# Pooled conditioning, attention and a mixture of experts on one core: block 0's first units weigh their rows last, weights come in 512 KB transfers, score banks are freed earlier, and the halves of the even blocks' input lie elsewhere

## What is computed

```python
# pooling of the tokens of a sequence; a mask of three kinds
scores = tanh(x @ W1 + b1) @ v
p = softmax(where(mask, scores[:, None, :], NEG_INF))
pooled = einsum('bjl,bld->bjd', p, x) / cnt
# attention, 16 heads of 8, one rope part of 32 for all heads
c_kv = pooled @ W_kv_down
k, v = c_kv @ W_k_up, c_kv @ W_v_up
k_rope = rotary(c_kv @ W_k_rope)
q, q_rope = pooled @ W_q, rotary(pooled @ W_q_rope)
w = softmax(causal((q k^T + q_rope k_rope^T) / scale))
x = x + (w @ v) @ W_o
# experts
xc = x @ W[cat_ids] + b[cat_ids]
tidx, tw = gate(xc)          # sigmoid, 4 of 8 groups, the best 8 of 64, normed, times 2.5
y = sum over e of cw[:, e] * ((silu(xc @ We_gate[e]) * (xc @ We_up[e])) @ We_down[e])
y = y + (silu(xc @ Ws_gate) * (xc @ Ws_up)) @ Ws_down
x = x + y
```

## Time and profile before

| | |
|---|---|
| median of 3 runs (lowest, highest) | 727.07 us (725.82, 727.83) |
| the profiled execution | 730.47 us |
| its span in the trace | 728.6 us |
| mean granted clock of PE | 0.988 |
| PE busy | 704.1 us (97%) |
| PEld busy | 547.9 us (75%) |
| DVE busy | 543.2 us (75%) |
| ACT busy | 444.0 us (61%) |
| POOL busy | 424.5 us (58%) |
| HBM read, written | 88.37 MB, 3.15 MB |

### The profile page before, as it was taken

How to read it: one execution, slowest core, us unless ns; L and a number is a source line. 1 busy time by engine, 2 the same in 40 slices (tenths; PEclk the granted TensorE clock), 3 DMA queues, 4 the chain that set the end, 5 groups by cost and what they waited for, 6 DMA issues and landing times.

```text
span 728.6 us, 15761 instructions
## 1 busy us (share of the span) xinstructions
PE 704.1 (97%) x5616; PEld 547.9 (75%) x5616; DVE 543.2 (75%) x1146; ACT 444.0 (61%) x857; POOL 424.5 (58%) x351
## 2 busy tenths in 40 slices
PE   7989889999999999999999999999999999999997
PEld 5767668677887778777787778877787777888885
...
GB/s 257 107 113 124 202 149 112 124 104 163 106 124 114 145 109 121 138 101 146 120 112 137 107 157 105 126 113 140 113 125 138 97 150 115 110 129 142 128 130 46
DMA packets 66845, 92.93 MB, mean 128 GB/s; under 512 B 7888, under 2 KB 26768, under 8 KB 66768
## 3 DMA queue, kind: packets, MB, share of 16 engines
...
HBM read 88.37 MB, written 3.15 MB: 126 GB/s over the span
## 4 chain that ended last, share of the span: by engine, by line
PE 74%; DVE 10%; ACT 5%; SPq 4%; issue 4%; DMA 2%; POOL 1%; POOLq 0%; DVEq 0%; ACTq 0%
PE banks L997 71%; DVE hid L964 3%; DVE hid L976 2%; PE banks L1077 2%; DVE k_blk L693 1%; DVE pt_sb L668 1%; SPq L302 1%; ACT banks L531 1%; SPq L296 1%; DMA x_early<-in_x_feat 1%; SPq L272 1%; ACT s_t L405 1%; ACT hid_hi L543 1%; SPq L333 1%; ACT v_blk L392 1%
## 5 line engine op out<-in xcount | busy, mean ns | idle before, releaser
L640 POOL TENSOR_TENSOR hid_lo<-hid,hid_hi 128x512 fp32r<-128x512 f32 (+1 forms) x264 | 342.1, 1296 | 261.1 <-ACT hid_hi L543 259.3
L964 DVE TENSOR_TENSOR hid<-banks,cwb 128x512 f32<-128x512 f32 x254 | 174.6, 687 | 122.1 <-ACT banks L531 115.1
L531 ACT ACTIVATE banks<-banks 128x512 f32<-128x512 f32 x254 | 147.4, 582 | 134.3 <-PE banks L997 132.7
L543 ACT CAST hid_hi<-hid 128x512 fp32r<-128x512 f32 (+1 forms) x264 | 162.7, 616 | 78.7 <-DVE hid L976 76.9
L976 DVE TENSOR_TENSOR hid<-hid,banks 128x512 f32<-128x512 f32 (+1 forms) x264 | 181.4, 687 | 25.3 <-PE banks L997 2.9
L997 PE MATMUL banks<-c_hi,wg_hi 128*128 128x512 f32 x264 | 118.9, 450 | 4.6 <-DVE hid L964 3.4
L997 PE MATMUL banks<-hid_hi,wd_hi 128*128 128x512 f32 (+1 forms) x264 | 104.6, 396 | 0.8 <-POOL hid_lo L640 0.8
L997 PE MATMUL banks<-c_hi,wg_lo 128*128 128x512 f32 x264 | 104.0, 394 | 0.0
L997 PE MATMUL banks<-c_lo,wg_hi 128*128 128x512 f32 x264 | 104.0, 394 | 0.0
L997 PE MATMUL banks<-hid_hi,wd_lo 128*128 128x512 f32 (+1 forms) x264 | 103.7, 393 | 0.0
L997 PE MATMUL banks<-hid_lo,wd_hi 128*128 128x512 f32 (+1 forms) x264 | 103.6, 393 | 0.0
...
## 6 DMA issues: line engine op xcount, KB each, us to landing
cwb<-cw_scratch SPq DMA_DIRECT2D x254, 256.0 KB, 3.8
...
xf<-in_x_feat SPq DMA_DIRECT2D x8, 256.0 KB, 3.9
out_feat<-y ACTq DMA_DIRECT2D x8, 256.0 KB, 3.4
wg_raw<-in_we_gate SPq DMA_DIRECT2D x7, 256.0 KB, 4.7
wu_raw<-in_we_up SPq DMA_DIRECT2D x7, 256.0 KB, 4.5
wd_raw<-in_we_down SPq DMA_DIRECT2D x7, 256.0 KB, 4.5
xf<-in_x_tok SPq DMA_DIRECT2D x6, 256.0 KB, 2.7
```

What stands on the lines that cost most here:

```text
L531: nc.scalar.activation(dst, gate_bank(p)[:, :], ACT.Silu).then_inc(S["silu_done"], 1)
L543: nc.scalar.copy(hid_hi[0:n, slot(b, p), :], hid[0:n, slot(b, p), :]).then_inc(S["hi_ready"], 1)
L640: nc.gpsimd.tensor_sub(hid_lo[0:n, slot(b, p), :], hid[0:n, slot(b, p), :], hid_hi[0:n, slot(b, p), :].bitcast(F32)).then_inc(S["lo_ready" ...
L964: nc.vector.tensor_mul(hid[:, slot(b, p), :], gate, weight)\
```

## The change

In eight parts:

1. **First loads.** `x_feat` 0 is second on SP's queue, was fourth. `consts` moves to ACT's. The seven other loads of `x_feat` and `x_tok` 1 move from ACT's queue to SP's.
2. **Weights in 512 KB.** `weight_pair` loads eight pairs of experts at once, 12 transfers in place of 24. ACT issues those of the first pair of quarters, SP seven more and the shared expert's ahead of block 0's units, and the last two down parts ahead of the first cwb. None stands between two cwb any more.
3. **Prologue order.** PE's `pool_scores(1)` goes from ahead of `pool_out(0)` to behind step 0, DVE's to step 5; ACT's splits 0 and 1 go to step 4; warming products are 5 and 2 where there were 2, 6 and 2, and 7 where there were 9.
4. **Rows weighed last in units 0 to 3 of block 0.** ACT puts silu 0 to 3 into `hid`; DVE multiplies by up first (`gate_up`) and by the weights second; the gates of units 2 and 3 stand ahead of the transposition of the weights, their ups behind the `pick` products. These go to Y and A1 (`first_bank`).
5. **Two tiles at once.** DVE (and POOL) do steps 6 and 7 behind unit 1 and 8 and 9 behind unit 3 (`TWO_TILES`); PE's step 8, the second round of scores, goes from unit 3 to unit 4 (`SECOND_ROUND`). `pool_weights(2)` goes from unit 6 to unit 5.
6. **Splits.** 8 in place of 10 ahead of the units; then one behind each of units 6 to 17, and 20 to 24 behind units 24 to 28. `CHAIN` goes from 25 to 21.
7. **Score banks.** A semaphore `score_read` at the addition of the mask (L714) replaces `biased_tile`, at the maximum (L715), in the waits of step 8, of the first transposition in step 12 and of up 6. Before, the addition and the maximum followed each other by a wait too.
8. **Address.** c_hi0 and c_lo0 are declared right behind `wd_hi`.

The diff, cut:

```diff
@@ -109,6 +109,7 @@
         hid_hi, hid_lo = sb("hid_hi", [P, NH, TOK], F32R), sb("hid_lo", [P, NH, TOK], F32R)
         wg_hi, wu_hi = sb("wg_hi", [P, UNITS, P], F32R), sb("wu_hi", [P, NPAIR, P], F32R)
         wd_hi = sb("wd_hi", [P, UNITS, D], F32R)
+        c_hi0, c_lo0 = sb("c_hi0", [P, TOK], F32R), sb("c_lo0", [P, TOK], F32R)
...
-        c_hi = [sb("c_hi0", [P, TOK], F32R), c_hi1]
-        c_lo = [sb("c_lo0", [P, TOK], F32R), c_lo1]
+        c_hi, c_lo = [c_hi0, c_hi1], [c_lo0, c_lo1]
...
+        first_bank = [Y, A1]
...
+        def steps_behind(p, b, prev, moved, last=False):
+
+            if not prev and p in moved:
+                return [(step, 1) for step in moved[p]]
+            return steps_in(p, b, last)
+
+        TWO_TILES = {0: [], 1: [6, 7], 2: [], 3: [8, 9], 4: []}
+        SECOND_ROUND = {3: [], 4: [8]}
...
-        BEFORE_UNITS = 10
-        SPLITS = {4: 10, **{p: p + 5 for p in range(6, 17)}, 26: 22, 27: 23, 28: 24}
-        CHAIN = 25
+        BEFORE_UNITS = 8
+        SPLITS = {**{p: p + 2 for p in range(6, 18)}, 24: 20, 25: 21, 26: 22, 27: 23, 28: 24}
+        CHAIN = 21
...
+        def weight_pair(k, m):
+
+            raw = (wg_raw, wu_raw, wd_raw)[m][:, 8 * k:8 * k + 8, :].rearrange("p a b -> p (a b)")
+            return raw, (we_gate, we_up, we_down)[m][:, bass.ts(k, 2 * TOK)]
...
@@ -256,20 +271,19 @@
         def _(sp):
             cond = W_COLS["kvT"][0]
             sp.dma_start(w[:, 0:cond], weights[:, 0:cond]).then_inc(S["cond_in"], 16)
-            sp.dma_start(c[:, :], consts).then_inc(S["consts_in"], 16)
+            sp.dma_start(xf_in[0], x_feat[:, bass.ts(0, TOK)]).then_inc(S["x_in0"], 16)
             sp.dma_start(pt_i, prompt).then_inc(S["prompt_in"], 16)
-            sp.dma_start(xf_in[0], x_feat[:, bass.ts(0, TOK)]).then_inc(S["x_in0"], 16)
             sp.dma_start(w[:, cond:], weights[:, cond:]).then_inc(S["proj_in"], 16)
             sp.dma_start(xt_in[0].rearrange("p (t d) -> p t d", d=D), x_tok[:, 0:TILES, :]).then_inc(S["xt_in0"], 16)
+            for i in range(1, 4):
+                sp.dma_start(xf_in[i], x_feat[:, bass.ts(i, TOK)]).then_inc(S["x_in1"], 16)
             sp.dma_start(cat_row[:, :], cats.to_broadcast([CATS, NSEQ])).then_inc(S["cats_in"], 16)
             sp.dma_start(cat_table, cond_b).then_inc(S["cats_in"], 16)
...
-            for i in range(3):
-                weight_load(i)
+            for i in range(4, NBLK):
+                sp.dma_start(xf_in[i], x_feat[:, bass.ts(i, TOK)]).then_inc(S["x_in2"], 16)
+            token_load(1, "xt_in1")
             sp.wait_ge(S["cats_in"], 48)
...
-            for i in range(6, 14):
-                weight_load(i)
+            for m in range(3):
+                weight_load(1, m)
+            for k in (2, 3):
+                for m in range(2):
+                    weight_load(k, m)
+            sp.dma_start(wg_raw[:, NPAIR, :], ws_gu).then_inc(S["ws_in"], 16)
+            sp.dma_start(wd_raw[0:F, NPAIR, :], ws_down).then_inc(S["ws_in"], 16)
+            sp.wait_ge(S["c2tok_ps"], 1)
+            for k in (2, 3):
+                weight_load(k, 2)
...
+                    if not prev and 2 + NCW <= p < 4 + NCW:
+                        sp.wait_ge(S["hid_ready"], p - NCW + 1)
+                    else:
+                        sp.wait_ge(S["weighted"], b * NPAIR + (NPAIR + p - NCW + 1))
...
-                if not prev and 2 <= p < 12:
-                    if p == 2:
-                        sp.wait_ge(S["c2tok_ps"], 1)
-                    weight_load(p + 12)
...
+            act.dma_start(c[:, :], consts).then_inc(S["consts_in"], 16)
...
-            for i in range(1, NBLK):
-                act.dma_start(xf_in[i], x_feat[:, bass.ts(i, TOK)]).then_inc(S["x_in1" if i < 4 else "x_in2"], 16)
             act.wait_ge(S["cond_in"], 16)
             act.wait_ge(S["consts_in"], 16)
             pool_hidden(0)
+            for m in range(3):
+                act.dma_start(*weight_pair(0, m)).then_inc(w_in[m], 16)
             pool_exp(0)
...
             pool_hidden(1)
-            for i in range(3, 6):
-                weight_load(i)
-            act.dma_start(xt_in[1].rearrange("p (t d) -> p t d", d=D), x_tok[:, bass.ts(1, TILES), :]).then_inc(S["xt_in1"], 16)
             pooled_out(0)
-            split(0)
-            split(1)
             for p in range(CWT):
                 attention_step(p, 0)
-                if p == 8:
+                if p == 4:
+                    split(0)
+                    split(1)
+                elif p == 8:
...
-                    dst = hid[:, p, :] if b == 0 and p < 2 else gate_bank(p)[:, :]
+                    dst = hid[:, p, :] if b == 0 and p < 4 else gate_bank(p)[:, :]
...
+                if not first or p < 2:
+                    silu(b, p)
                 if p == 1 and not prev:
+                    silu(b, 2)
+                    silu(b, 3)
                     attention_step(CWT, 0)
                     attention_step(CWT + 1, 0)
+                if first and p == 3:
+                    attention_step(p + AHEAD, 1)
+                    steps = []
...
-                if 12 <= p < 17:
+                if 10 <= p < 17:
...
-                    chain(nc.vector.tensor_add(s, ps, bias), blk)
+                    nc.vector.tensor_add(s, ps, bias).then_inc(S["score_read"], 1)
+                    dve.wait_ge(S["score_read"], blk * TILES + t + 1)
...
-            pool_scores(1)
...
+                if p == 5:
+                    pool_scores(1)
+                elif p == 9:
                     pool_weights(1)
...
+            def gate_up(p):
+
+                dve.wait_ge(S["silu_done"], p + 1)
+                dve.wait_ge(S["up_done"], p + 1)
+                nc.vector.tensor_mul(hid[:, p, :], hid[:, p, :], U[p % 2]).then_inc(S["weighted"], 1)
...
+                if first and p < 2:
+                    dve.wait_ge(S["cwb_ps"], p + 1)
+                    up = first_bank[p]
+                elif first:
+                    dve.wait_ge(cwb_in[p % NCW], 16)
+                    up = cwb[:, p % NCW, :]
                 nc.vector.tensor_mul(hid[0:n, slot(b, p), :], hid[0:n, slot(b, p), :], up).then_inc(S["hid_ready"], 1)
-                if not prev and p == 6:
+                if not prev and p == 1:
+                    gate_up(2)
+                    gate_up(3)
+                elif not prev and p == 5:
                     pool_weights(2)
...
-                        pe.wait_ge(S["biased_tile"], blk * NG + 2)
+                        pe.wait_ge(S["score_read"], blk * NG + 2)
...
@@ -1188,15 +1219,15 @@
             pe.wait_ge(S["proj_in"], 16)
             first, width = W_COLS["k"][0], 2 * D + 2 * ROPE
             mm(A2[:, 0:width], W["kvT"], w[:, first:first + width]).then_inc(S["fold_ps"], 1)
+            warm(5)
             pool_hidden(1)
             warm(2)
-            pool_scores(1)
-            warm(6)
             pool_out(0)
             pe.wait_ge(S["setup"], 2)
-            warm(2)
             first_products(0)
             for p in range(CWT):
+                if p == 1:
+                    pool_scores(1)
                 attention_step(p, 0)
...
-                warm(9, Y)
+                warm(7, Y)
...
-                pe.wait_ge(S["silu_done"], 2)
+                pe.wait_ge(S["k_ready"], 2 * HG)
                 pe.wait_ge(S["pick_ready"], 1)
                 for u in range(2):
-                    dst = G[u].rearrange("p (u two n) -> p two u n", two=2, n=P)
+                    dst = first_bank[u].rearrange("p (u two n) -> p two u n", two=2, n=P)
...
+                elif b == 0 and p in (2, 3, 4, 5):
+                    pe.wait_ge(S["silu_done"], p - 1)
...
+                elif b == 0 and p in (2, 3, 4, 5):
+                    pe.wait_ge(S["weighted"], NPAIR + p - 1)
...
                 elif not prev and p == 1:
                     attention_step(5, 1)
+                    for q in (2, 3):
+                        gate(b, q, par, following)
                     first_weights()
+                    for q in (2, 3):
+                        up(b, q, par, following, prev)
```

91 lines of the change are left out of this document (41 added, 50 removed).

## The result

The changed kernel takes 724.12 us in the median of its runs, the kernel before 727.78; the ratio is 0.9951, with a 95% interval from 0.9937 to 0.9964. By the medians the change makes the kernel 3.7 us (0.5%) faster. I had forecast 12.6 us (714.5, range 709 to 720). The sign was right, the size was not. One of the changed kernel's twenty executions took 970.25 us at a mean granted clock of 0.656; the ratio leaves it out, and the other nineteen took 720.55 to 728.15 (median 723.95).

A forecast was written before the change was run, and what follows sets the result against it. Until about 107 us a relay (first activations, expert weights, SP's queue, clock) bounds the kernel, then PE. 4.7 + 5.5 + 1.7 - 0.9 + 1.6 = 12.6 off 727.07 gives 714.5 us, range 709 to 720.

The forecast's parts named there:

- leg 1: Prologue up to gate 0: earlier first activations start the attention products 5.9 earlier; 4.7 us gained net, bounds 2.5 and 6.
- gate 0 to T: Block 0, gate 0 to the transposition of the weights (T): gates 2 and 3 now stand ahead, making it 1.0 late.
- T to A: Block 0, weights' transposition to that ahead of block 1's output product: SP's queue no longer binds; 6.5 us less.
- A to block 1: clock: Behind the transposition ahead of block 1's output product: the half-clock stretch from 97 to 101.5 goes; 1.7 us gained.
- A to block 1: splits: End of block 0: splits 20 and 21 in units 24 and 25 make split 22, which gate 28 needs, 0.9 later.
- blocks 1 to 6: Address of c_hi0 and c_lo0, moved from 179 to 123 KB: half of a possible 3.2, so 1.6 us with block 0.
- rival 1: Prologue gives less: activation loads 1 to 3 share engines with ACT's weights, PE drops to half clock; 717.0 us, chance 0.18.
- SP no longer binds: Block 0, units 5 to 12: without weight loads between cwb, unit 11's cwb is issued at 82; ACT and DVE limit next.
- The two weightings from SBUF: Block 0, units 2 and 3: DVE's weighting reads two SBUF inputs while POOL subtracts; 0.5 us lost.
- The sign that I gave for the transposition, 85.7: Check on the transposition before wo, ahead of block 1's output product: near 85.7 instead of 96.38.
- the 0.89 between even and odd blocks: Block 2 takes 85.33 us, block 3 84.44; the 0.89 was put down to reading c_hi0 and c_lo0 from the far place.
- Rival 3: New place of c_hi0 and c_lo0 as fast as 54 KB, DVE under 2.6 a unit: 710.6 us, chance 0.13.

The follow-up runs named there:

- the two second profiles: The kernel before and the changed kernel, both unchanged, each profiled once more: 727.00 and 724.02 us (one run each).
- the residual first: Changed kernel with SP issuing block 0's residual load (xf) ahead of x_feat 4 to 7 and the register and category loads: 720.34 us, 0.9898 of before.
- two other profiles of the old prologue: The kernel before profiled again (727.00 us), and the kernel before with only c_hi0 and c_lo0 declared behind wd_hi (725.77 us).
- the registers early: Changed kernel with SP reading block 1's categories into registers ahead of block 0's units, not behind units 4 to 7: 722.92 us.
- the kernel with three edits: Changed kernel with residual load ahead of category loads, block 1's registers read ahead of the units, splits 20 to 24 behind units 18 to 22: 719.82 us, 0.9905 of before.
- the two profiles with full clock: Changed kernel with block 1's registers read ahead of the units (722.92 us), and changed kernel with splits 20 to 24 behind units 18 to 22 (724.77 us).
- equal code with full clock: Changed kernel with splits 20 to 24 behind units 18 to 22, the same code up to unit 17: 724.77 us.

## Why the prediction was wrong

Of the two second profiles (727.00 and 724.02, 2.98 apart) the parts are:

| part | forecast | measured |
|---|---|---|
| leg 1, to gate 0 | 4.7 | 42.91 - 42.85 = 0.06 |
| gate 0 to T | -1.0 | 8.60 - 11.04 = -2.44 |
| T to A | 6.5 | 42.91 - 35.16 = 7.75 |
| A to block 1: clock | 1.7 | -1.6 |
| A to block 1: splits | -0.9 | -2.0 |
| blocks 1 to 6 | (1.6 with block 0) | 505.97 - 504.70 = 1.27 |
| sum | 12.6 | 3.0 |

The line on the clock is the 52.26 of the residual first, which has no half clock there, less 53.86; the line on the splits is 50.26 less 52.26.

**Leg 1 failed: 4.7 forecast, 0.06 measured, so 4.6 of the 9.6 that are missing between these profiles (8.9 by the medians).** Two things went wrong in it. The first is a step that wasn't there: I followed the attention's chain to gate 0 and did not ask what else gate 0 needs. It needs the residual's load, behind sixteen category loads in SP's row. In the trace of before SP issues xf at 32.46, it lands 3.3 later, and the addition stood at 39.54; so at most 3.7 us were open in that execution, and in two other profiles of the old prologue none. The change did not bring that load forward (issued at 34.08 and 31.98 in its two profiles, at 32.46 and 32.65 in those of before). My rival 1 looked at the right queue for the wrong load. The second is the base: against the profile that I read, the leg's own steps were right, landing near 5.4 (5.04), first products at 13.7 (13.54), output product 4.7 earlier (4.54). Between the second profiles the first products are 3.6 earlier (16.64 and 13.05) and the output product only 1.92.

**A single profile was taken as the kernel's normal state.** The execution was 3.4 above the median, and I knew it; I took the 3.4 off the end and left the parts as they were. But most of it sat in a part: gate 0 at 45.96 for 42.91. What is slow in an unusual execution can't be gained in the usual one.

**Block 0, units 0 to 12: right.** The transposition of the weights comes 0.83 later by itself (1.0 forecast; with a half clock it was 2.25 and 2.44 in the two profiles). From T to A I had worked out 35.3 us (90.4 and 0.5, less 55.56), and it took 35.35 and 35.16. What that gains depends on the profile of before: 6.5 between the first ones, 7.75 between the second ones, where the kernel before had half clock from 62 to 70 and from 82 to 88. In the parts there were errors. The cwb of unit 11 goes out 24.7 after the first, not 22.6, since the four category loads with their cwb take 2.9 to 3.5 a unit and not 2.6; SP is then late for units 10 and 11, where DVE waits 0.34 and 1.31. "SP no longer binds" is so only with the registers early, and there DVE takes from unit 8 to A the 10.4 that I had worked out. The two weightings from SBUF took 0.68 and 0.84 in the changed kernel, so the 0.5 for them was 0.2 here; in the residual first one took 1.54, in the kernel with three edits one took 1.84. The sign that I gave for the transposition, 85.7, leaves the 0.5 out; with it the sum gives 86.2.

**The clock: a term that one profile could not give.** I had taken one half-clock stretch away and put none in its place, though the change leaves PE waiting 2.36, 0.85, 0.63, 1.81 and 2.27 at five places (the residual, gates 2, 3, 7 and 28). Two of them could be read from the plan: gates 2 and 3 need a silu that ACT has just begun. Behind A both profiles of the changed kernel lose 1.6 where I had a gain of 1.7. But the stretch of the earlier trace rows isn't in the second profile of before either, where others are (about 8 to 12, 52 to 56, 62 to 70 and 82 to 88), and the waits don't decide alone, as the two profiles with full clock show. Over all executions the sign is the other one: the mean granted clock is 0.990 in 66 executions of the kernel before and 0.993 in the changed kernel's nineteen. As an estimate from these and the spans, with 0.5 as the low level, that is some 14 and 10 us at half clock; what it costs depends on whether PE sets the pace there. The Trainium skill, "TensorE: Matmul & The Clock Gate" (Part 1: The HAM clock gate), says of one kernel's start that the number of products at the low clock varied from run to run. The profiles here show the like in mid-kernel: gate 16 of the changed kernel at 100.45 and 98.20, and at 96.21 in equal code with full clock, of which 0.9 is the landing of one load. Such a term belongs into the range, not into the sum.

**Splits: half seen.** 0.9 of the 2.0 was forecast, for gate 28 (1.2 measured). The 1.2 at units 20 and 21 was not (0.4 comes back over the rest of the stretch): I had called the splits of units 6 to 17 covered by POOL's spare time, and did not look at what runs beside them on DVE.

**Address: right by luck.** 1.6 forecast as half of 3.2, and 1.27 measured in blocks 1 to 6. It is not a half: it is the whole effect in blocks 2, 4 and 6, less what blocks 3 and 5 lose at DVE; and the 0.89 between even and odd blocks held both.

Of the rivals none was the case. Rival 1 names the prologue, but not the residual. Rival 3 is half right: the new place is as fast as 54 KB, but that was not worth 1.6 more.

What stays open: where the half clock falls in and why, 3.3 of the 9.6 in the profiles, and whether any order of the warming products prevents it.
